# Attention row sums on Trainium2: the last 16 keys added on VectorE and GpSimd in place of a masked product on TensorE

## The reference, cut to what matters

```
scores = exp(-(q2[:, None] + k2[None, :] - 2 * Q K^T))     # 400 queries x 400 keys, per image
attn   = softmax(scores, axis=-1)                          # exp(scores) / sum over keys of exp(scores)
out    = attn V                                            # 400 queries x 32 channels, per image
```

## Time and profile before

| what | value |
|---|---|
| median of 3 runs | 228.37 us |
| profiled execution: its own time | 227.03 us |
| its span, first to last instruction | 225.2 us |
| mean granted TensorE clock | 0.967 |
| TensorE matmul busy | 198.7 us (88%) |
| ScalarE busy | 169.5 us (75%) |
| VectorE busy | 161.3 us (72%) |
| GpSimd busy | 28.7 us (13%) |
| attention units (first to last score) | 79.8 to 180.5 us of the span |

### The profile page before, as it was taken

One profiled execution on the slowest core, in us unless ns is written; L12 is line 12 of the kernel. 1 busy time (PEld: TensorE's weight loads), 2 busy tenths in 40 slices (PEclk: granted clock), 3 DMA queues, 4 the chain that ended last, 5 costly groups with the idle time before them and its releaser, 6 DMA issues. The chain is left out here.

```text
span 225.2 us, 3444 instructions
## 1 busy us (share of the span) xinstructions
PE 198.7 (88%) x1182; PEld 98.1 (44%) x1182; DVE 161.3 (72%) x294; ACT 169.5 (75%) x307; POOL 28.7 (13%) x44
## 2 busy tenths in 40 slices
PE   6858999999999597889799999999999998599960
PEld 6633655646546244323234343434343423276640
DVE  0649279989989724994958495968777795585980
ACT  4073798799696779988988989899999964365540
POOL 7000000550320080070101010101010000000000
PEclk9999999999999889969999999999999999979995
DMA  6950200395998085399623526080800000000016
GB/s 172 355 172 6 73 1 0 95 339 156 285 286 270 2 283 175 124 322 232 182 45 102 119 56 168 6 219 0 222 0 3 0 0 0 0 3 3 0 48 246
DMA packets 26885, 26.87 MB, mean 119 GB/s; under 512 B 1550, under 2 KB 25806, under 8 KB 26740
## 3 DMA queue, kind: packets, MB, share of 16 engines
q1 hardware_dynamic: 26868, 26.64, 40.6%
HBM read 14.74 MB, written 11.88 MB: 118 GB/s over the span
## 5 line engine op out<-in xcount | busy, mean ns | idle before, releaser
L511 ACT ACTIVATE arena<-ps 128x800 f32<-128x800 f32 (+1 forms) x56 | 44.5, 797 | 6.7 <-PE ps L1067 4.6
L518 ACT ACTIVATE arena<-arena 128x800 f32<-128x800 f32 (+1 forms) x56 | 46.4, 830 | 0.0
L1067 PE MATMUL ps<-qa,ka 128*128 128x400 bf16 (+1 forms) x128 | 35.6, 342 | 2.0 <-ACT arena L511 1.9
L1067 PE MATMUL ps<-qb,kb 96*128 96x400 bf16 (+1 forms) x128 | 35.4, 339 | 0.0
L743 DVE TENSOR_TENSOR psum<-arena 128x400 f32<-128x400 f32 x32 | 19.6, 611 | 13.5 <-ACT arena L518 13.5
L743 DVE TENSOR_TENSOR psum<-psum,arena 128x400 f32<-128x400 f32 x32 | 19.5, 609 | 7.8 <-ACT arena L518 6.4
L1100 PE MATMUL ps<-arena,vb 128*32 128x400 f32 x192 | 21.6, 525 | 1.1 <-issue 1.1
L1067 PEld LDWEIGHTS ps<-qa,ka 128*128 128x128 bf16 (+1 forms) x128 | 10.4, 98 | 26.3 <-ACT arena L511 13.7
L752 DVE RECIPROCAL arena<-ps 128x400 f32<-128x400 f32 x7 | 18.5, 2649 | 0.0
L662 DVE COPY arena<-arena 32x400 f32<-32x400 f32 x48 | 17.2, 358 | 0.9
L1184 PE MATMUL ps<-yb,cst 128*128 128x160 f32 x72 | 17.1, 333 | 0.0
(11 more groups left out here) (148 smaller groups left out, 359.7 us busy)
## 6 DMA issues: line engine op xcount, KB each, us to landing
dka<-arena SPq DMA_DIRECT2D x16, 200.0 KB, 3.0
dqa<-arena SPq DMA_DIRECT2D x16, 200.0 KB, 3.2
ka<-dka SPq DMA_DIRECT2D x8, 400.0 KB
qa<-dqa SPq DMA_DIRECT2D x8, 400.0 KB
arena<-x_tok SPq DMA_DIRECT2D x4, 400.0 KB
t<-x SPq DMA_DIRECT2D x1, 1600.0 KB, 11.9
dkb<-arena SPq DMA_DIRECT2D x8, 200.0 KB, 3.6
dqb<-arena SPq DMA_DIRECT2D x8, 200.0 KB, 3.9
```

What stands on the lines that cost most here:

```text
L511: nc.scalar.activation(prob[par][:, lo:hi, :], ps[:, o:o + hi - lo, 0:N], ACT.Exp, scale=2.0).then_inc(e1_done, 1)
L518: nc.scalar.activation(p, p, ACT.Exp).then_inc(p_ready, 1)
L1067: last = mm_(ps[row:row + keys, bank, 0:N], kk[par][0:rows, b, o:o + keys], qq[par][0:rows, b, :], start=first, stop=not first, skip_group ...
```

## The change

The tail of each group but the last is now added into the partial sums in SBUF before the sums product. GpSimd does it for images 0 and 1 (`POOL_TAILS = 2`): it multiplies rows 0 to 63 of tile 12 by a 0/1 column (`in_tail`, built once from `tail_ones` by four small copies) into `masked`, which lies in the output buffer of group 0, and adds the two 32-row parts to `psum`. VectorE does it for images 2 and 3, with one `scalar_tensor_tensor` of 32 partitions each. On VectorE this stands behind the additions of unit 1 of the next group. TensorE's `sums` waits for both, moves from unit 3 to unit 4, and ends its accumulation itself; `tail_sums` stays only for the last group. `reciprocals` moves from unit 2 to unit 3, and waits for the sums product; `quotient` and `residual` move from unit 4 to unit 5 (in the last group from unit 2 to unit 3). GpSimd's loop over groups is written out, without the wait of `apart` (which had long been met).

```diff
+            def add_tails(g, par):                       # GpSimd
+                pool.wait_ge(vb_ready, min(g + 2, G))
+                pool.wait_ge(p_ready, UNITS * (g + 1))
+                rows = slice(0, C * POOL_TAILS)
+                nc.gpsimd.tensor_tensor(masked[rows, :], prob[par][rows, TILES - 1, :],
+                                        in_tail[rows, :].to_broadcast([C * POOL_TAILS, N]), ALU.mult).then_inc(masked_ready, 1)
+                pool.wait_ge(masked_ready, g + 1)
+                pool.wait_ge(part_sum, ADDS * (g + 1))
+                for b in range(POOL_TAILS):
+                    rows = slice(C * b, C * b + C)
+                    nc.gpsimd.tensor_tensor(psum[rows, par, b, :], psum[rows, par, b, :], masked[rows, :],
+                                            ALU.add).then_inc(tail_added, 1)
+                    pool.wait_ge(tail_added, POOL_TAILS * g + b + 1)
+            for g in range(G - 1):
+                add_tails(g, g % 2)
+                if g + 2 < G:
+                    pool.wait_ge(pv_done, g + 1)
+                    values(g + 2, g % 2)
...
+            def add_tails(g, par):                       # VectorE
+                dve.wait_ge(p_ready, UNITS * (g + 1))
+                dve.wait_ge(part_sum, ADDS * (g + 1))
+                for b in range(POOL_TAILS, NB):
+                    rows = slice(C * b, C * b + C)
+                    nc.vector.scalar_tensor_tensor(out=psum[rows, par, b, :], in0=prob[par][rows, TILES - 1, :],
+                                                   scalar=c_("tail_ones")[rows, C * b:C * b + 1],
+                                                   in1=psum[rows, par, b, :],
+                                                   op0=ALU.mult, op1=ALU.add).then_inc(tail_added2, 1)
             def reciprocals(g, first=False):
-                dve.wait_ge(sums_done, g + 1)
+                dve.wait_ge(psum_used, g + 1)
...
-                    if since > 0 and u == 2:
+                    if since > 0 and u == 1:
+                        add_tails(g - 1, 1 - par)
+                    if since > 0 and u == 3:
                         reciprocals(g - 1, first=since == 1)
...
-                    if since > 0 and u == (4 if g < G - 1 else 2):
+                    if since > 0 and u == (5 if g < G - 1 else 3):
                         quotient(g - 1, first=since == 1)
                         residual(g - 1)
...
             def sums(g, par, first):                     # TensorE
-                pe.wait_ge(part_sum, ADDS * (g + 1))
+                if g < G - 1:
+                    pe.wait_ge(tail_added, POOL_TAILS * (g + 1))
+                    pe.wait_ge(tail_added2, (NB - POOL_TAILS) * (g + 1))
+                else:
+                    pe.wait_ge(part_sum, ADDS * G)
...
-                    if since > 0 and u == 3:
+                    if since > 0 and u == 4:
                         sums(g - 1, 1 - par, first=since == 1)
-                        tail_sums(g - 1, 1 - par)
```

More of the change, by code:

```diff
@@ L196, in build @@
         log_ready = sem("log_ready")
+        tail_added, tail_added2, masked_ready, mask_set = (
+            sem(n) for n in ("tail_added", "tail_added2", "masked_ready", "mask_set"))
         bn_c, bn_pe, bn_act, primed, cmp_c, cmp_pe, flag_ok, added = (
@@ L208, in build @@
         OUT_G = 2
+        POOL_TAILS = 2
+        masked = outs[:, 0, :]
+        in_tail = col(38)
         WARM_FIRST, WARM = 10, 2
@@ L393, in _ @@
                 square_parts(i)
[L395 to L399, removed]
+            def add_tails(g, par):
[11 more added lines that the diff above has]
+                    pool.wait_ge(tail_added, POOL_TAILS * g + b + 1)
+            pool.wait_ge(e_ready, PAIRS + CREDIT1)
+            for b in range(NB):
+                rows = slice(C * b, C * b + C)
+                nc.gpsimd.tensor_copy(in_tail[rows, :], c_("tail_ones")[rows, C * b:C * b + 1]).then_inc(mask_set, 1)
+                pool.wait_ge(mask_set, b + 1)
+            for g in range(G - 1):
[3 more added lines that the diff above has]
+                    values(g + 2, g % 2)
         @block.scalar
@@ L534, in last_reciprocals @@
             def last_reciprocals():
[L536 removed]
+                act.wait_ge(sums_done, 1)
                 act.wait_ge(nrm_ready, G - 1)
@@ L1077, in sums @@
                 for b in range(NB):
-                    last = mm_(ps[C * b:C * b + C, 5, 0:N], c_("ones"), psum[:, par, b, :], start=True, stop=False,
-                               skip_group_check=True)
+                    last = mm_(ps[C * b:C * b + C, 5, 0:N], c_("ones"), psum[:, par, b, :], start=True,
+                               stop=g < G - 1, skip_group_check=True)
                 last.then_inc(psum_used, 1)
```

## The result

The changed kernel takes 234.38 us in the median (4 runs, 232.67 to 236.62), against 227.92 us for the kernel before, timed again beside it. The ratio is 1.0297, with a 95% interval of 1.0242 to 1.0353: it is slower by 3%. Forecast were 233.6 us, in a range of 229 to 239.

What follows compares the result with a forecast made beforehand. TensorE was taken as the bound (11.99 of 12.00 us busy), ScalarE close behind. A later start, five periods of 12.95 us and the end gave +5.2 us: 232.2 us profiled, 233.6 us median, range 229 to 239.

Steps and rivals of the forecast that it cites:

- The wait and its loop: TensorE's moved sums wait for VectorE's tails behind unit 1; period 12.95 us against 11.97, +0.98 us a group.
- Forecast parts 0.81, 5.09, 5.15 and 1.9: Sums to centering; centering to next unit 0's exponential; to unit 1's second exponential's end; VectorE's addition, two tails, step.
- The second rival: ScalarE's unit 6 and next unit 0 never wait for TensorE after the stall; period 12.2, 229.8 us; chance 0.17.
- The removed product: Masked product leaves TensorE in 7 groups: 0.78 us each, at most 0.6 obtainable; the gain vanishes in TensorE's new wait.
- The quotient's move: VectorE's quotient moves from unit 4 to 5; its loop, 12.5 us, is 0.45 shorter, costing nothing except at the start.
- the first rival: No stall: tails done before TensorE reaches the sums, ScalarE's 11.38 us sets the pace; 4.2 us saved, 224.2 us; chance 0.10.
- GpSimd off the path: GpSimd's three instructions per group, 2.8 to 3.5 us plus short waits, end 2 us or more before VectorE's tails.
- The third rival: GpSimd's instructions slip and hold up a VectorE tail; up to 0.94 us a loop, +4.7 us, 238.3 us; chance 0.15.
- The size: Last sums start at 189.7 instead of 184.50, +5.2 us; profiled execution 232.2 us, median 233.6 us.
- the second sums: TensorE's second sums start at 117.8, 3.6 us later than 114.18.
- TensorE's branch of the last group's sum: In the last group TensorE, freed by the quotient, needs 0.1 and 0.8 + 0.7 + 0.8 us; last sums at 189.7.

Runs made afterwards that it cites:

- both edits together: The changed kernel with VectorE's tails behind unit 0 instead of unit 1, and quotient and residual back behind unit 4: 229.35 us, ratio 1.0082.

## Why the prediction was right

- *The wait and its loop.* Right in place, cause and size. Forecast parts 0.81, 5.09, 5.15 and 1.9, measured 0.81, 5.09, 5.15 and 2.03; the 0.13 is the tails' 1.29 us for two instead of 1.2. Moving the tails away from unit 1 took the wait off (12.12), doubling VectorE's added what the loop says (14.21 against 13.08), taking the centering out took 0.77 off (12.31), and leaving GpSimd's part out changed next to nothing (13.03). The second rival, in which ScalarE catches up, failed where the prediction said: ScalarE still waits for TensorE in units 5, 6 and 0 (0.18, 0.25 and 0.32 us).
- *The removed product.* Right that its 0.78 us would be lost in the wait. That 0.6 us a group could be had at most was too much: 0.36 in the mean, with nothing put in its place.
- *The quotient's move.* The result was right (no cost beside the longer loop: 13.07 and 13.08 with and without it), the working was not, so this part came right by luck: both the 12.5 us that I had and the true 12.12 lie under the tails' loop. I followed VectorE's own chain from the tails. The loop that binds goes through TensorE's order: first product to unit 6's scores 8.45 us (135.81 to 144.26 in the run with tails behind unit 0), then 0.60 to ScalarE's unit 6, 0.40, 0.86 for unit 5's second exponential, VectorE's two additions 1.14 and quotient 0.57, and 0.1: 12.12 us, as measured. So with the tails out of the way the changed order still costs, which the first rival (224.2 us without a stall) did not see.
- *GpSimd off the path.* Right with two images (2.3 us early by the trace; 13.03 without it). It took no loss on the path but at the first sums: there two tails lasted 1.96 us instead of 1.29 while GpSimd added. Beside the path its price was larger than I had it: residual 1.27 us instead of 0.57, additions 1.23 instead of 0.94, and VectorE busy 11.31 of 13.08 us where I had said 10.5. The third rival, collisions that reach the tails, came true with three images on GpSimd.
- *The size.* From the row of 103.15 or 104.74 on, the last sums moved by 192.71 - 184.50 - 1.59 = 6.6 us; I had 5.2. The 1.4 between are the second sums 0.55 later than worked out, five periods of 0.13, and 0.2 in the last group. The median moved by 6.5. That its level is off by only 0.8 is in part luck: the kernel before stood at 228.37 when I wrote and at 227.92 when timed again.
- *Two slips that change nothing.* TensorE's branch of the last group's sum gives 189.8, not 189.7. And the trace of before has a second stretch at a clock of 0.50, from 197 to 200 us, behind the attention.

## What to carry to other kernels

When an engine is full only because all engines go in step, ask for each instruction moved or added which closed loops through the written orders it lies in, and add up each loop: the longest is the new period, and the others decide what mending it brings. Here the tails' loop had 13.1 us, and in another place still 12.2; the quotient's had 12.1 and the crowded stretch 12.0. They lay within about 1 us, so undoing one edit showed only the next. Price the removal with nothing in its place first: it was worth about 1 us, and in that order no way of doing the work elsewhere could have brought more. No version with the tail additions came out under the kernel before.

## What the runs showed of the hardware

- VectorE and GpSimd, both on instructions that read two tensors of SBUF (or one and a column), took turns: 1.29 us instead of 0.57 for an addition, 1.31 instead of 0.65 for a tail. It went the other way round too: with both edits together GpSimd's multiplication, begun at 146.89 during an addition of VectorE that kept its 0.57, took 1.15 us instead of 0.85. Instructions of VectorE with one input in PSUM kept their time beside GpSimd: the reciprocal at 135.01 its 2.65 us and the second normalization's product at 129.77 its 0.87. The Trainium skill ("SBUF — State Buffer", section "Who interferes with whom") has both halves of this, two SBUF inputs exclude GpSimd's reads and one does not; the traces agree.
- A multiply-add of VectorE on 32 partitions x 400 costs 0.65 us, no less than an addition on 128 partitions (0.57).
- TensorE's clock stayed at 1.00 in the steady part of the changed kernel, with waits of 0.93 and 0.89 us in each period of 13.08. With all tails on VectorE, where a period of 14.21 has waits of 2.07 and 0.89, it fell to 0.50 (1.2 GHz) in two of the five steady periods, which then lasted 15.9 us, and in the first period, behind a wait of 2.22.
